# Taking the second list's tiles of a mixture of experts in the order full, full, half instead of all half tiles last

## The reference

```python
scores = jax.nn.sigmoid(xf @ gate_w + bias)
top_scores, top_idx = jax.lax.top_k(scores, K)            # K = 2 of E = 8 experts
...
up = jnp.einsum('th,ehi->tei', xf, up_w) + up_b           # h = 128, i = 512
hact = jax.nn.gelu(up, approximate=False)
eo = jnp.einsum('tei,eih->teh', hact, down_w) + down_b
combined = jnp.einsum('teh,te->th', eo * 0.1, w)
shared = (jax.nn.gelu(xf @ sw_up + sb_up, approximate=False) @ sw_down + sb_down) * 0.1
```

## Time and profile before

| | us |
|---|---|
| median of the 3 runs shown (688.51 to 694.85) | 694.38 |
| the profiled execution | 694.08 |
| its span, first to last instruction | 692.4 |
| PE busy | 646.9 (93%) |
| PEld busy | 439.9 (64%) |
| ACT busy | 480.7 (69%) |
| DVE busy | 433.7 (63%) |
| POOL busy | 395.0 (57%) |

### The profile page before, as it was taken

The page is one execution under the profiler, slowest core; times in us unless marked ns, Lnnn a source line. Parts: engine busy times, 40 slices in busy tenths (PEclk is TensorE's granted clock), DMA queues, the critical chain, the costliest instruction groups (busy, mean ns, idle before and its releaser), DMA issues.

```text
span 692.4 us, 11700 instructions
## 1 busy us (share of the span) xinstructions
PE 646.9 (93%) x3699; PEld 439.9 (64%) x3699; DVE 433.7 (63%) x999; ACT 480.7 (69%) x763; POOL 395.0 (57%) x558
## 2 busy tenths in 40 slices
PE   7998999999999989999997999898989999999994
PEld 5565555656565546469886999875566665555642
DVE  2674686687878788754632654213569888787663
ACT  4865798787988686686443555543889897978563
POOL 5435467578788787812542455154676777725353
PEclk9996999999999999999999999999999999999998
DMA  8066660000000000058887687711111100000003
GB/s 238 10 234 256 246 246 5 24 10 19 17 18 19 26 26 20 24 164 244 254 249 217 171 251 234 226 39 31 32 31 31 30 27 27 16 0 16 15 2 92
DMA packets 66777, 66.46 MB, mean 96 GB/s; under 512 B 7378, under 2 KB 49707, under 8 KB 66715
## 3 DMA queue, kind: packets, MB, share of 16 engines
q1 hardware_dynamic: 60448, 52.62, 25.1%
q0 software_dynamic: 6208, 13.07, 5.8%
q10 hardware_dynamic: 58, 0.02, 0.0%
HBM read 37.31 MB, written 27.85 MB: 94 GB/s over the span
## 4 chain that ended last, share of the span: by engine, by line
PE 38%; POOL 9%; issue 9%; DVE 7%; DMA 6%; ACT 5%; SPq 1%; POOLq 1%; DVEq 0%; ACTq 0%
PE PS L1183 7%; POOL got L2097 4%; PE PS L1163 3%; PE PS L1259 2%; DMA got<-expert_rows,IU 2%; PE PS L975 2%; PE PS L1041 2%; PE PS L1083 2%; POOL H L2028 2%; PE PS L981 1%; DMA expert_rows<-five,IU 1%; PE PS L987 1%; DMA XT<-expert_rows 1%; PE PS L1170 1%; PE PS L1171 1%
## 5 line engine op out<-in xcount | busy, mean ns | idle before, releaser
L1923 ACT ACTIVATE GF<-PS,XN 128x256 f32<-128x256 f32 (+1 forms) x156 | 68.5, 456 | 62.2 <-PE PS L1163 29.6
L2069 POOL DMA_INDIRECT expert_rows<-five,IU x64 | 63.8, 997 | 40.4 <-DMA expert_rows<-five,IU 18.8
L2097 POOL DMA_INDIRECT got<-expert_rows,IU x64 | 64.1, 1002 | 39.7 <-DMA got<-expert_rows,IU 22.4
L1183 PE MATMUL PS<-WD,GF 128*128 128x128 f32 x568 | 83.4, 276 | 0.9 <-ACT GF L1923 0.9
L1401 DVE TENSOR_REDUCE MX<-PS 128x4 f32<-128x896 f32 (+2 forms) x96 | 61.2, 685 | 30.1 <-PE PS L1046 29.2
L1183 PEld LDWEIGHTS PS<-WD,GF 128*128 128x128 f32 x568 | 75.5, 193 | 2.5 <-ACT GF L1923 1.3
L1884 ACT ACTIVATE PA<-PS 128x1024 f32<-128x1024 f32 x64 | 64.9, 1038 | 11.1 <-PE PS L1067 10.9
L2058 POOL TENSOR_SCALAR_AFFINE_SELECT PA<-PA 128x256 f32<-128x256 f32 x128 | 50.6, 426 | 14.3 <-ACT PA L1884 14.2
L2028 POOL TENSOR_SCALAR H<-xc,MOD 128x256 f32<-128x256 f32 x56 | 32.7, 592 | 39.3 <-DVE xc L1366 38.8
L2082 POOL DMA_DIRECT2D expert_rows<-YT x39 | 21.7, 557 | 57.6 <-issue 37.6
L1163 PE MATMUL PS<-XS,WU 128*128 128x256 f32 (+1 forms) x192 | 47.1, 357 | 4.8 <-DVE XS L1648 4.7
(11 more groups left out here) (337 smaller groups left out, 1754.5 us busy)
## 6 DMA issues: line engine op xcount, KB each, us to landing
expert_rows<-five SPq DMA_DIRECT2D x16, 1024.0 KB, 9.0
WU<-in_L_ffn_up_w SPq DMA_DIRECT2D x39, 256.0 KB
WD<-in_L_ffn_down_w SPq DMA_DIRECT2D x39, 256.0 KB
XT<-expert_rows SPq DMA_DIRECT2D x32, 128.0 KB
expert_rows<-YT POOLq DMA_DIRECT2D x32, 128.0 KB, 3.5
BD<-in_L_ffn_down_b SPq DMA_DIRECT2D x39, 64.0 KB
PA<-in_L_attn_x SPq DMA_DIRECT2D x8, 256.0 KB, 5.3
out<-yo SPq DMA_DIRECT2D x8, 256.0 KB, 2.6
```

Source lines behind the costliest of these rows:

```text
L1183: m = pe.matmul(bk[:, b], g[:, b], wd[:, k, :], start=(k == 0 and t == 0), stop=(k == 3 and t == blocks - 1))
L1923: act.activation(GF[slot["gf", kind, u, k]][:, 0:n], bank("up", kind, u, k)[:, 0:n], ACT.Gelu, bias=bias).then_inc(sems["gelu"], 1)
L2069: pool.indirect_dma_start(out=XD[:, :], out_offset=bass.IndirectOffsetOnAxis(ap=IU[:, c, n, k:k + 1], axis=0), in_=HT[c % 2][:, k, :], in_ ...
L2097: pool.indirect_dma_start(out=got[b][n][:, k, :], out_offset=None, in_=XD[:, :], in_offset=bass.IndirectOffsetOnAxis(ap=IU[:, c, n, k:k + ...
```

## The change

The second list keeps its 15 full and 7 half tiles, but takes two full ones and then a half one: full are 17, 18, 20, 21, 23, 24 and so on to 35, 36 and 38; half are 19, 22, 25, 28, 31, 34 and 37. A fixed table, ENTRY, says which row of the plan a tile number uses; the plan itself is computed as before. Where the code asked the number of the tile, it now asks the table. ORDER1 is untouched.

```diff
+def entries():
+    full, half, mixed = list(range(N1, NP)), list(range(NP, NT)), []
+    while full or half:
+        mixed += full[:2] + half[:1]
+        full, half = full[2:], half[1:]
+    return list(range(N1)) + mixed
+
+ENTRY = entries()
+
 def rows(t):
-    return TR if t < NP else HALF
+    return TR if ENTRY[t] < NP else HALF
+
+def parted(t):
+    return N1 <= t and ENTRY[t] < NP
...
     def weights_in(t, ahead=()):
-        if t >= NP:
+        if t >= NT or not parted(t):
             return
...
-                if not N1 <= u < NP:
+                if not parted(u):
...
-            if not N1 <= t < NP:
+            if not parted(t):
...
-            bias = vec("L0_ffn_sb_up", k) if kind == "s" else UB[:, u, k:k + 1]
+            bias = vec("L0_ffn_sb_up", k) if kind == "s" else UB[:, ENTRY[u], k:k + 1]
...
-            row = pool.value_load(EI[0:1, 1, t:t + 1], min_val=0, max_val=E * CAP)
+            row = pool.value_load(EI[0:1, 1, ENTRY[t]:ENTRY[t] + 1], min_val=0, max_val=E * CAP)
...
-            ex = sp.value_load(EI[0:1, 0, t:t + 1], min_val=0, max_val=E - 1)
+            ex = sp.value_load(EI[0:1, 0, ENTRY[t]:ENTRY[t] + 1], min_val=0, max_val=E - 1)
...
-            row = sp.value_load(EI[0:1, 1, t:t + 1], min_val=0, max_val=E * CAP)
+            row = sp.value_load(EI[0:1, 1, ENTRY[t]:ENTRY[t] + 1], min_val=0, max_val=E * CAP)
```

## The result

Of 22 executions each, the median is 695.12 us (691.02 to 699.37) with the change and 694.46 us (684.40 to 699.57) before. The ratio is 1.0047, with a 95% interval of 1.0027 to 1.0067: slower by 1.9 to 4.7 us by this measure, and within 1%. It counts fast executions alone, those within 1.5% of their kernel's fastest, and since one execution before took 684.40 us, nine of the 22 before fall out by this and none with the change. Over all 22 each, the means (695.6 and 694.0 us) differ by 1.6 us and the medians by 0.7, so how much slower the change is must be read from the stretch that it changed.

A forecast was written before the change was run, and what follows sets the result against it. Late rows at the half tiles, from SyncE's fetch issue, bound the kernel. WO path (-3.96 + 4.2 = +0.2 us) against fetches (+1.3): the later, plus 0.1 and 0.3, gave +1.7 and 696.0 us, range 690.0 to 699.5.

The forecast's parts named there:

- What bounded the kernel: Half tiles ending the second list: rows late; a fetch costs SyncE's queue 3.22 us against 1.89 us of work.
- Waits removed: Half tiles at the second list's end: 3.96 us of TensorE's waits go if the transfers keep up.
- The WO chain: Full tiles behind half ones: TensorE stalls for WO, made on GpSimd behind a store; 0 to 4.2 us added.
- The fetch clock: SyncE's queue in the second list: last fetch issues at 444.2 us, 0.7 us earlier than before.
- The later of the two clocks counts: Second list's end: later of WO path (+0.2 us) and fetches (+1.3 us) counts; WO stalls hide in waits for rows.
- the waits for rows that I gave as a sign: Second list, 430 to 450 us: TensorE would wait for rows at tiles of both sizes.
- The tail: Last tile, now full: landed rows to YT take 5.98 us instead of 4.05; YT starts at 455.8 us, +1.3.
- One for one to the end: Behind the second list: a delay of the last store counts one for one to the kernel's end.
- A: Rival, chance 0.22: in the second list only the WO chain counts, the queue sticks less; 695.0 us.
- B: Rival, chance 0.13: full gain in the second list, transfers keep up and WO has more slack; -3.6 us, 690.8 us.
- C: Rival, chance 0.07: transfers of the second list fall behind, last fetch 8.0 us later; 704.8 us.
- The size: Whole kernel: first gather +1.7 us, forecast 696.0 us against a median of 694.38; chance 0.50.

The follow-up runs named there:

- run 5: Order of before, but one value load per fetch instead of two (expert worked out from the row), against the kernel before: list 61.36 us, ratio 0.9939.
- run 6: Mixed order with WO made ahead of the store and one value load per fetch, against the kernel before: list 59.87 us, ratio 0.9917.
- run 2: Mixed order without the bias load from tile 23 on, against the kernel before: list 64.80 us, ratio 1.0016.
- Run 7: Mixed order shifted by one so that a half tile is last, against the kernel before: list 64.12 us, ratio 1.0002.
- Run 1: Mixed order with WO made ahead of the store beside it on GpSimd, against the kernel before: list 66.16 us, ratio 1.0037.
- run 8: Mixed order with half tile last, WO ahead of the store and one value load per fetch, against the kernel before: list 59.87 us, ratio 0.9945.
- run 3: Mixed order with WO ahead of the store and no bias load from tile 23 on, against the kernel before: list 59.87 us, ratio 0.9932.

## Why the prediction was right, point by point

- **What bounded the kernel.** Right. The rows came late for the half tiles, by issue of the queue: runs 5 and 6 took issue and no bytes, and the waits went from 3.3 to 1.3 us and to none. The order changed too in run 6, so run 5 is the cleaner of the two.
- **Waits removed, 3.96 us.** Right in size: run 6's list is 63.79 - 59.87 = 3.92 us shorter than before.
- **The WO chain, 4.2 us.** The mechanism was right, the term was too small. The six rounds are over 8.75 us by 0.70, 0.71, 1.02, 0.70, 0.74 and 1.33, together 5.2 us. Four of them are WO waits of 0.70 to 0.74, where I had 0.35 + 0.29 = 0.64; in the third round the store of tile 24 was issued 0.3 us later than elsewhere (in runs 2 and 7 too; why stays open), and the last has waits for rows in it. (The list of waits has only 1.6 us, since the modelled ends of the matmuls cover the rest; the starts of the weight loads show it.) I had counted the slack as 0.42 us, up to the load of the weight. But 0.12 us of it is the hop from GpSimd to TensorE, as the changed kernel shows: WO ends at 389.27, the load starts at 389.39. The stalls there are 0.45 and 0.28 us.
- **The fetch clock, last WU issue 51.8 us behind the first.** 52.20. Right, the long issues recurred: 1.25, 1.41 and 1.43 us. But the reading that backed it was wrong: "no window of ten microseconds is over 276" GB/s holds from 290 us on, where I had read them. Earlier the same kernel moves 367 and 387 GB/s in two windows of five (shown in the last section), where SyncE issues stores of 1024 KB. So 276 is no ceiling of this kernel, and that a round asks 277 GB/s gave no ground to expect the transfers to fall behind.
- **The later of the two clocks counts, stalls on WO hide in the waits for rows.** This step was only half right, and the forecast came near partly by luck. I had the fetches last, at +1.3 us, and the WO chain at +0.2. Run 2, in which the fetches are never late, puts the WO chain alone at 64.80 us, +1.0, and the changed kernel at +1.68: the fetches add 0.67 to it. At tiles 20 to 35 TensorE had no wait for rows; it waited for those of tiles 36 and 37, in the round of 10.08 us. The weight loads of their transposes show it:

```profile
438.44 0.20 PEld L1164 LDWEIGHTS PS<-CT,XT 128*128 128x128 f32 x2 [0.46 <-DMA XT<-expert_rows]
...
441.87 0.14 PEld L1164 LDWEIGHTS PS<-CT,XT 128*128 128x128 f32 x1 [0.25 <-DMA XT<-expert_rows]
```

  These two, together 0.7 us, are what came of the waits for rows that I gave as a sign. Run 1 is the fetch clock alone and gives no less.
- **The tail.** The last tile's path, from rows to YT, was put at 5.98 us; it is 451.25 - 444.91 = 6.34. The store of tile 35 stands ahead of the last WO, which I had left out of the sum:

```profile
445.11 0.54 POOL L2097 DMA_DIRECT2D expert_rows<-YT  x1 [3.35 <-issue]
445.67 1.29 POOL L2090 TENSOR_TENSOR WO<-WU,WH 128x512 fp32r<-128x512 f32 x1
...
452.87 0.54 POOL L2097 DMA_DIRECT2D expert_rows<-YT  x1 [1.71 <-issue]
455.76 1.02 POOL L2112 DMA_INDIRECT got<-expert_rows,IU  x1 [2.35 <-DMA expert_rows<-YT]
```

  WH was through at 445.34, but WO started at 445.67, behind the store, which started 1.63 us behind its YT as at tile 17. So it was the WO chain that ended last here too, not the fetch: from tile 35's YT to tile 38's it is 7.77 us, and 7.77 in run 2, whose WH did not wait. The sum by the fetch path comes out only 0.4 us short since two of its three errors cancel: last WU issue +0.4 us, landing 5.20 us instead of 5.56, path 6.34 instead of 5.98. YT to gather is 4.51 us against 4.19, +0.32, where I had +0.43. Run 7 puts what a full last tile costs at 0.7 us.
- **One for one to the end.** Right in every profile: from the first gather to the end of the span it is 232.4 to 233.7 us.
- **The rivals.** A is what the stretch looks like up to tile 32, but not its time. B needed two edits more (run 6), and then its price held: 3.6 us less to the gather (67.98 to 64.37). C did not come; the last WU issue stayed 51.3 to 52.6 us behind the first in every run that issues all that the kernel before does. The page "DMA: Bandwidth & Descriptors" of the Trainium skill, section Specifications, has the limit on the HBM side at about 358 GB/s. The second list stays under it: bandwidth was not the clock at 230 to 253 GB/s, which the forecast had doubted, and run 8 had 273 GB/s over 40 us. But the figure is no limit for this kernel: from 55 to 60 us the traces have 385 to 388 GB/s, and the measurement decides.
- **The size.** Forecast 696.0 against 694.38, +1.6 us. The medians of 22 runs differ by 0.7 and the means by 1.6, the ratio says 3.3 (1.9 to 4.7), and the stretch in the profiles 2.0.

## What to carry to other kernels

Mixing cheap and dear tiles evens out a queue's load, but every chain that is made ready "one tile ahead" loses the difference of the two tiles' lengths as slack: here 0.3 us of slack stood against 0.77 for the first full tile behind a half one. Two clocks of nearly equal length must be loosened together: alone, the two edits moved the list by +0.7 and -0.7 us, together by -5.6. Count the instructions of an issuing queue and not only its bytes: a value that can be worked out from another one need not be loaded.

## What I had not expected

**The start of the second list moves by 10 us between executions, ahead of any changed code.** YT of tile 17 starts between 385.05 and 394.71 us in the ten profiles. Part of it goes with one stretch early in the kernel. Windows of the kernel before, then of the changed one (columns as in the earlier trace rows):

```profile
50.00:55.00 5.00, 2.70 (x17) 2.01 (x16) 1.29 (x2) 2.58 (x6) 3.99 (x11) 0.82 1.04 367
55.00:60.00 5.00, 5.00 (x19) 4.04 (x19) 1.89 (x3) 3.12 (x4) 1.43 (x4) 0.50 1.03 387
```

```profile
60.00:65.00 5.00, 5.00 (x24) 1.96 (x27) 2.19 (x4) 2.63 (x4) 2.42 (x4) 0.50 0.75 281
65.00:70.00 5.00, 5.00 (x40) 2.91 (x32) 2.47 (x5) 4.00 (x7) 3.04 (x7) 0.81 0.01 3
```

```profile
50.00:55.00 5.00, 2.81 (x18) 2.23 (x18) 1.29 (x2) 2.99 (x5) 3.99 (x11) 1.00 1.03 365
55.00:60.00 5.00, 4.95 (x33) 2.83 (x32) 3.44 (x6) 4.65 (x7) 3.22 (x6) 1.00 1.03 388
```

Before, TensorE's granted clock is 0.82, then 0.50 until 65 us, the lower of its two levels (1.2 of 2.4 GHz), then 0.81; in the five microseconds in which it fell TensorE had been busy for 2.70 us. In the other execution it had been busy for nearly the same, 2.81 us, and the clock stayed at 1.00. The first of the two is about 5 us behind from there on: its first tile's copy starts at 305.84 us, the other's at 300.40. Of the ten profiles, the four with a mean clock of 0.86 from 50 to 100 us have that copy at 303.6 to 306.9 us, the four with 1.00 at 298.0 to 300.5; run 3 (0.93) has it at 300.8 and run 8 (0.90) at 305.6. This spread is larger than the effect of the change, so one profile's span says nothing about it. Why the clock fell in one execution and not in the other stays open.

**An issue of SyncE's queue sometimes takes 0.86 to 1.95 us, as at 398.29, 415.20 and 429.67 in the changed kernel, instead of 0.33 to 0.4**, two to four times in the 16 fetches of every run, at any of the four transfers, with 230 GB/s as with 273. What holds it was not settled: it came no more often when the fetches went faster (two and three times in runs 6 and 8).
